# Attention, routing scores and experts in one block of engine programs, and the experts' parts added ahead of the shared part in 20 tiles

## What is computed

```python
x = layernorm(x + attention(x))              # 16 heads of 32, softmax over 1024 keys
scores = x @ gate_w.T                        # 8 experts
ew, ei = top_k(scores, 2); ew = softmax(ew)
routed = sum over the 2 chosen experts of ew * (silu(x @ w_gate.T) * (x @ w_up.T)) @ w_down.T
shared = (silu(x @ sh_gate.T) * (x @ sh_up.T)) @ sh_down.T
x = layernorm(x + routed + sigmoid(x @ se_gate_w.T) * shared)
```

## Time and profile before

| | us |
|---|---|
| median of 3 runs (2097.38 to 2098.63) | 2098.14 |
| the profiled execution | 2099.2 |
| its span, first to last instruction | 2097.5 |
| PE busy | 2018.8 (96%) |
| DVE busy | 1278.3 (61%) |
| ACT busy | 880.3 (42%) |
| POOL busy | 868.1 (41%) |
| granted TensorE clock, mean share of full | 0.988 |

### The profile page before, as it was taken

How to read it: one execution, slowest core, us unless ns; L and a number is a source line. 1 busy time by engine, 2 the same in 40 slices (tenths; PEclk the granted TensorE clock), 3 DMA queues, 4 the chain that set the end, 5 groups by cost and what they waited for, 6 DMA issues and landing times. The chain is left out here.

```text
span 2097.5 us, 30323 instructions
## 1 busy us (share of the span) xinstructions
PE 2018.8 (96%) x9764; PEld 1226.9 (58%) x9765; DVE 1278.3 (61%) x2281; ACT 880.3 (42%) x1563; POOL 868.1 (41%) x831
## 2 busy tenths in 40 slices
PE   7999999999999999999999986899999999999997
PEld 5655556655556655556655435588544444447886
DVE  5777775777776677775677855574222222225875
ACT  2266664466664466663466672321111111112332
POOL 3255654556654556653554555200111111114651
PEclk9999999999999999999999998999999999999999
DMA  7322434331434231335131305642222222225752
GB/s 231 71 53 55 100 78 107 115 69 42 101 76 131 92 76 47 97 67 163 60 77 33 91 12 201 221 186 66 90 90 88 86 87 89 90 80 166 229 175 74
DMA packets 95923, 213.00 MB, mean 102 GB/s; under 512 B 24305, under 2 KB 24817, under 8 KB 92593
## 3 DMA queue, kind: packets, MB, share of 16 engines
q1 hardware_dynamic: 84992, 175.96, 28.3%
q0 software_dynamic: 10800, 35.40, 6.2%
HBM read 118.51 MB, written 41.93 MB: 76 GB/s over the span
## 5 line engine op out<-in xcount | busy, mean ns | idle before, releaser
L947 DVE TENSOR_REDUCE max_half<-ps_side 128x1 f32<-128x512 f32 x1024 | 658.2, 682 | 204.6 <-PE ps_side L666 201.4
L666 PE MATMUL ps_side<-kq_stack 96*128 96x512 f32 x1024 | 409.4, 404 | 4.9 <-DVE max_half L947 2.4
L688 PE MATMUL ps_s<-kq_stack 97*128 97x512 f32 x937 | 393.0, 420 | 8.0 <-ACT probs_first L843 5.1
L688 PEld LDWEIGHTS ps_s<-kq_stack 97*128 97x128 f32 x937 | 177.8, 190 | 165.0 <-issue 85.5
L1636 PE MATMUL ps_gu<-gu_sb,xT_e 128*128 x568 | 257.7, 596 | 0.5 <-issue 0.3
L1534 POOL DMA_INDIRECT x_g<-x,who_all x71 | 67.3, 948 | 454.7 <-PE ps_t L1626 358.4
L843 ACT ACTIVATE probs_first<-ps_s 128x512 f32<-128x512 f32 x326 | 187.6, 600 | 106.0 <-PE ps_s L688 90.5
L666 PEld LDWEIGHTS ps_side<-kq_stack 96*128 96x128 f32 x1024 | 195.2, 191 | 57.8 <-DVE max_half L947 26.5
L843 ACT ACTIVATE probs_mid<-ps_s 128x512 f32<-128x512 f32 x308 | 177.5, 599 | 112.0 <-PE ps_s L688 97.4
L590 POOL TENSOR_TENSOR acc<-probs_first,probs_mid 128x512 f32<-128x512 f32 x129 | 163.8, 1297 | 133.2 <-ACT probs_mid L843 133.2
L843 ACT ACTIVATE probs_last<-ps_s 128x512 f32<-128x512 f32 x303 | 175.5, 599 | 97.2 <-PE ps_s L688 81.0
(11 more groups left out here) (237 smaller groups left out, 3312.0 us busy)
## 6 DMA issues: line engine op xcount, KB each, us to landing
kq_stack<-kq SPq DMA_DIRECT2D x192, 256.0 KB, 5.1
y_slots<-y_t SPq DMA_DIRECT2D x71, 256.0 KB, 2.3
x_r<-x SPq DMA_DIRECT2D x32, 256.0 KB, 3.7
x_t<-x SPq DMA_DIRECT2D x32, 256.0 KB, 2.9
gu_sb<-wgu SPq DMA_DIRECT2D x8, 1024.0 KB, 16.1
out<-gu_sb SPq DMA_DIRECT2D x32, 256.0 KB, 2.7
res<-inv_rows SPq DMA_DIRECT2D x124, 64.0 KB, 2.0
stage<-wkqT SPq DMA_DIRECT2D x28, 256.0 KB, 3.0
```

What stands on the lines that cost most here:

```text
L666: nc.tensor.matmul(bank, q_stack[par][0:3 * HD, h, t * P:(t + 1) * P], k_stack[par][0:3 * HD, h, half * HALF:(half + 1) * HALF], start=Tru ...
L688: nc.tensor.matmul(out, k_stack[par][0:3 * HD + 1, h, kt * P:(kt + 1) * P], q_stack[par][0:3 * HD + 1, h, half * HALF:(half + 1) * HALF], ...
L947: nc.vector.reduce_max(max_half[:, u // 2, u % 2:u % 2 + 1], bank, AX.X).then_inc(side_free, 1)
```

## The change

All of attention, scores and experts is put into one block: one program per engine, with no barrier between stages, and one identity matrix. What was in the block of the scores and now has to share memory with the attention became a class `Router`. Its buffers lie where those of `feed_forward` lie later.

Work that moves into the attention's last group and tail: POOL clears `rw_raw`; SP loads the kept projection weights (now into `kq_stack0`, at the start of group 3 in place of the end of group 1), `rw` and tiles 0 to 3 of x2; in the tail PE turns tiles 0 to 7, ACT and DVE split them, SP loads tiles 4 to 11 and the three shared weights. SP's orders in the last group and the tail:

```diff
+            def load_last(b):
+                sp.wait_ge(scores_ready, b * HEADS_B + (G - 1) * STEPS * HG)
+                sp.sem_inc(passed, 1)
+                for i, part in enumerate(wo_last):
+                    sp.dma_start(part.bitcast(F32), wo_kept[i]).then_inc(wo_in, 16)
+                sp.wait_ge(router.rw_zero, 1)
+                sp.dma_start(router.rw_raw[:, :, 0:E + 1], router.rw).then_inc(router.rw_in, 16)
+                for t in range(4):
+                    sp.wait_ge(x2_out[t], 16 * 2)
+                    load_r(t)
             def body(b, m, g, last):
+                if last and g == G - 1:
+                    load_last(b)
...
-                if last and g == 1:
-                    sp.wait_ge(proj_ready, PROJ * B * G)
-                    sp.sem_inc(passed_sp, 1)
-                    for i, part in enumerate((x_hi, x_lo)):
-                        sp.dma_start(part[:, :, 0:D].bitcast(F32), wo_kept[i]).then_inc(wo_in, 16)
...
+                sp.wait_ge(scores_ready, B * HEADS_B)
+                sp.sem_inc(passed, 1)
+                load_shared(0)
+                for t in range(3):
                     store(b, t)
+                for t in range(4, 8):
+                    sp.wait_ge(router.t_ready, t - 3)
+                    load_r(t)
+                    if t < 7:
+                        store(b, t - 1)
+                for t in range(8, 12):
+                    sp.wait_ge(router.t_ready, t - 3)
+                    load_r(t)
+                for t in range(6, KT):
+                    store(b, t)
+                for k in range(1, 3):
+                    load_shared(k)
+                for t in range(12, TT):
+                    if t >= (B - 1) * KT:
+                        sp.wait_ge(x2_out[t % KT], 16 * (B + 1))
+                    sp.wait_ge(router.t_ready, t - 3)
+                    load_r(t)
```

PE, ACT and DVE in the tail of the last batch, and the scores' groups, which no longer turn tiles 0 to 7:

```diff
             for t in range(KT):
                 o_tile(b * TAIL + KT + t, b, t, tail_bank(t),
-                       [x_hi[:, g, 0:D] for g in range(G)], [x_lo[:, g, 0:D] for g in range(G)])
+                       [wo_last[0][:, g, :] for g in range(G)], [wo_last[1][:, g, :] for g in range(G)])
...
+                if 3 <= t < KT - 1:
+                    router.turn(pe, 0, t - 3)
+            for s in range(4):
+                router.turn(pe, 1, s)
+            pe.wait_ge(tail_free, B * TAIL)
...
             for t in range(KT):
                 norm(B - 1, t)
+                if 1 <= t < 5:
+                    router.high(act, 0, 0, t - 1)
+                if t >= 5:
+                    for s in ((0, 1), (2, 3), ())[t - 5]:
+                        router.high(act, 1, 1, s)
...
+                if 3 <= t < KT - 1:
+                    router.low(dve, 0, 0, t - 3)
+            for s in range(4):
+                router.low(dve, 1, 1, s)
...
             def group(q, g, first, last):
+                if not first and not last:
+                    for s in range(4):
+                        r.turn(pe, q + 1, s)
```

In the experts' block SP loads its first four tiles while the scores still run, and the experts' weights (12 MB) when the last tile is turned; `up(0)` and `down(0)` wait for the split shared weights:

```diff
             for t in range(4):
+                sp.wait_ge(router.t_ready, TT - 3 + t)
                 load_tile(t)
+            sp.wait_ge(router.st_split, 3 * C)
+            sp.sem_inc(passed, 1)
...
+                if t == 0:
+                    pe.wait_ge(router.st_split, 2 * C)
```

In the last 20 tiles DVE adds both experts' rows to x first (`begin_combine`), in the step before the shared part is there, and then adds the shared part (`finish_combine`) straight from PSUM; `finish` and its buffer fall away for these tiles:

```diff
+            def begin_combine(t):
+                dve.wait_ge(x_in[t % 4], 16 * (t // 4 + 1))
+                add_experts(t, x_t[:, t % 4, :]).then_inc(begun, 1)
+
+            def finish_combine(t):
+                q = COMBINE_AT[t]
+                s = q % 4
+                dve.wait_ge(d_ready, t + 1)
+                dve.wait_ge(begun, t - COVER + 1)
+                nc.vector.scalar_tensor_tensor(out=res[:, s, :], in0=ps_d[:, t % 2, :], scalar=sgate_all[:, t:t + 1],
+                                               in1=res[:, s, :], op0=ALU.mult, op1=ALU.add).then_inc(added, 1)
+                statistics(q)
...
                 if i:
-                    finish(t - 1)
+                    finish_combine(t - 1)
                 h_low(t)
-                for what in COMBINE_STEPS[i]:
-                    combine(*what)
-            finish(TT - 1)
-            for what in COMBINE_STEPS[TT - COVER]:
-                combine(*what)
+                if i < COVER:
+                    combine_stored(i)
+                begin_combine(t)
+            finish_combine(TT - 1)
```

More of the change, by code:

```diff
@@ new lines, in __init__, with turn @@
+        self.x_in = [sem(f"xr_in{i}") for i in range(4)]
+        self.t_ready, self.t_hi, self.t_lo = sem("r_t_ready"), sem("r_t_hi"), sem("r_t_lo")
+        self.sc_ready, self.sc_taken = sem("sc_ready"), sem("sc_taken")
+        self.back_ready, self.sc_done = sem("back_ready"), sem("sc_done")
+        self.th_done, self.gate_done = sem("th_done"), sem("gate_done")
+    def turn(self, pe, q, s):
+        t = 4 * q + s
+        pe.wait_ge(self.x_in[s], 16 * (q + 1))
+        if not static(q, 1):
+            pe.wait_ge(self.t_hi, t - 3)
+            pe.wait_ge(self.t_lo, t - 3)
+        for c in range(C):
+            done = self.nc.tensor.transpose(self.ps_t[:, s, c * P:(c + 1) * P], self.x_t[:, s, c * P:(c + 1) * P],
+                                            self.ident[:])
+        done.then_inc(self.t_ready, 1)
@@ L1169, in _ @@
         def _(pe):
-            def turn(q, s):
-                t = 4 * q + s
-                pe.wait_ge(x_in[s], 16 * (q + 1))
-                if not static(q, 1):
-                    pe.wait_ge(t_hi, t - 3)
-                    pe.wait_ge(t_lo, t - 3)
-                for c in range(C):
-                    done = nc.tensor.transpose(ps_t[:, s, c * P:(c + 1) * P], x_t[:, s, c * P:(c + 1) * P], ident[:])
-                done.then_inc(t_ready, 1)
             def score(q, g):
@@ L1203, in group @@
             def group(q, g, first, last):
+                if not first and not last:
+                    for s in range(4):
+                        r.turn(pe, q + 1, s)
                 if first:
-                    for s in range(4):
-                        turn(q, s)
-                if not last:
-                    for s in range(4):
-                        turn(q + 1, s)
-                if first:
-                    pe.wait_ge(rw_split, 1)
+                    pe.wait_ge(r.rw_split, 1)
                 score(q, g)
@@ L1265, in group @@
             def group(q, g, first, last):
-                if first:
-                    low(q, g)
-                if not last:
-                    low(q + 1, 1 - g)
+                if not first and not last:
+                    for s in range(4):
+                        r.low(dve, q + 1, 1 - g, s)
                 take(q, g)
```

414 lines of the change are left out of this document (208 added, 206 removed).

## The result

The changed kernel takes **2083.38 us** (median of 5, 2078.27 to 2088.77) against 2098.63 in the same session: ratio 0.993, 95% interval 0.9907 to 0.9952, so 15.3 us faster where I had forecast 19.7. The median lies 0.4 us above the top of my range. The single times spread over 10.5 us, where the kernel before had spread over 2.4 (in the three later sessions it spread over 10.3, 8.8 and 5.6 itself). In microseconds the two intervals are 10.1 to 19.5 and 14.5 to 21.4 faster: my 19.7 lies just outside the first and inside the second, so the times alone can't tell which step of the forecast was off. The traces have to.

The account below looks back on a forecast made before the run. PE was taken to bound the kernel, with time to win only where it stands or runs at its lower clock. Gains of 14.1 + 4.3 + 0.5 + 0.8 = 19.7 off 2098.1 gave 2078.4 us, range 2073 to 2083.

Parts of the forecast that it names:

- D: Last 20 tiles, additions in a new order: shorter end, `h_low` of the last tile later; gain 0.8 us, bounds 0 and 1.6.
- What bounds the kernel: Whole kernel: PE is busy nearly throughout, so time comes off only where it stands still or runs at its lower clock.
- A: Tail of the attention to the third scoring group's end: eight tiles turned early; gain 14.1 us, bounds 11 and 19.
- B: End of the scores to up(0): tile already loaded, PE turns it at once; gain 4.3 us, bounds 1.7 and 4.3.
- C: Clock of up(0): it has just fallen when up(0) starts; gain 0.5 us, bounds 0 and 2.5.
- clock holds at up(0): At up(0): the clock does not fall, 2 us more gain, 2076.4 us; chance 0.24.
- slower rival: Last 20 tiles: stores landing at 8 us make `begin_combine`'s wait eat 25 us, 2103.5 us; chance 0.03.
- the longer wait: Tail of the attention: tile 12's load takes the full 10.1 us, gain there 11, 2081.5 us; chance 0.14.

Follow-up runs that it names:

- shift_pe: Changed kernel with 20 idle waits on PE alone ahead of the experts' loop; 2081.2 us, run once.
- late_turns: Changed kernel with turns, copies and subtractions of tiles 0 to 3 moved behind the attention's last projection, loads still early; 2084.12 us, ratio 0.9938.
- shift_act: Changed kernel with 20 idle waits on ACT alone ahead of the experts' loop; 2079.34 us, run once.
- combine_only: Kernel before the change with only the new order of the additions in the last 20 tiles; 2098.19 us, ratio 0.9995.

## Why the prediction was off, step by step

Two steps failed: part D, which left out what the longer wait does to the clock, and the experts' loop, which the sum put at nothing without a reason.

**What bounds the kernel** was read rightly: the gain lies where PE stood, and there it was found.

**A and B** together were put at 14.1 + 4.3 = 18.4. The profiled execution has 18.06, the eight traces with this tail 15.2 to 18.4, mean 17.3. The way there: the last norm ended at 1287.2 and not 1289.6, since ACT's waits for POOL ahead of the norms, 1.2 to 1.9 us each before the change, absorbed its extra copies; tile 7 was turned at 1285.2 and not 1287.7. The wait for tile 12 then was 4.19 us and not 3.0. I had the load on PE 8.8 us after the first of the two 1 MB issues, 1.2 us less than the 10.1 of before. It came 10.2 us after it (1287.60 to 1297.85), so that saving did not show in this trace, and it ate half of what came earlier ahead of it. The clock fell behind the wait, as the row had it. In this trace the turns start at 1297.85 (forecast 1298.9), and the third group's last product ends at about 1304.2 (1305.8); but 2.2 us of PE's lead were there before the tail, so A itself is near 13.5. B is right: from the last turned scores to up(0) 2.05 us, 2.0 forecast.

**C** was put at 0.5 with 2.5 as its bound, and both cases come, in one kernel: 0.85 in eight of twelve traces, 2.45 in four. "Has just fallen" costs less than I took from the one row. The rival "clock holds at up(0)" was real but moves the time by 1.6 us, not 2.

**D is the first step that failed.** I gave +0.8, bounds 0 and 1.6. I had the 1.6 us of the shorter end and the 0.8 us by which `h_low` comes later, and counted the latter as delay alone. But it lengthens PE's wait from 1.46 to 2.25 us, and behind that the clock falls, in seven of the nine traces with this order: another 1.6 us (1.2 in shift_pe, where it rose sooner), so -0.72. In late_turns and shift_act the clock held, and there D is +0.86 and +0.85, my figure. In part A I had priced a wait with the clock behind it; here I did not.

**The loop is the second: the sum left it at nothing.** The experts' loop, not named in it, lost 1.8 to 2.3 us in every joined program whose DVE code was not moved, 2.07 in the first: outside my sum, and larger than the D error of 1.5. The wait for stores in `begin_combine`, my slower rival, never showed: PE's time in the steps from the third to the last but one is that of before within 0.03 us. (That rival's time should read 2078.4 + 25 = 2103.4.)

**The account.** Against one execution: 18.06 + 2.45 - 2.07 - 0.72 for the change, +2.85 for what that execution of the kernel before had by itself, -1.47 in the second of the last 20 steps, of which it is open whether the change or that execution has it, and -0.65 in the attention, makes 18.4. Over the eight traces with this tail the change alone is about 17.3 (A, B) + 1.45 (C, mean) - 2.1 (loop) - 0.7 (D) = 16.0, between the 15.3 and 16.5 of the two sessions; were the second step's mean loss of 1.1 the change's own, it would be 14.9. Against my 19.7 that is: A and B -1.1, C +0.9, loop -2.1, D -1.5. The kernel before is no fixed mark either: combine_only, with its old tail, is 1.84 behind in A and B. My range took its slow end from A alone (the longer wait, 2081.5, and 1.5 of uncertainty), at 2083.0. The loop lay outside it, and D's loss outside D's bounds. That the first median missed the range by only 0.4 us is chance: executions differ by more.

**The spread** of 10 us: the mean granted clock of the five first runs falls from 0.995 (2078.27) to 0.991 (2087.9 and 2088.77). Time at the 1.2 GHz level is 2 (1 - clock) of the span, half of it lost; so 0.004 more of it is up to 8.3 us of the 10.5, an estimate (the clock is rounded to 0.001, which is 2 us, and time at the lower level in which PE stands costs nothing). Which places fall in the slowest executions is not known, as they have no profile. Those seen falling in some traces and holding in others are around 1015, at tile 16, at up(0) and in the last tile.

## What to carry to other kernels

When an edit makes TensorE's wait longer by under a microsecond near a place where the clock may fall, price the clock too: here 0.8 us of statistics in front of one subtraction cost 2.4. A transfer that ended a wait before will take back part of what is won ahead of it, so look what stands in front of it on the queue. Before a sum is made from one profiled execution, mark the stalls that a second one might not have, and after a change that moves all the code compare the loops it "does not touch" instruction by instruction.

## What had not been expected of the hardware

- The clock does not fall alike in equal situations. After the same 2.25 us wait before the last products it fell in seven traces and held in two; at up(0), after the same 1.46 us wait and the short transposes before it, it fell in eight and held in four. At 1240 it fell behind a wait of 3.0 us and held behind one of 2.7.
- DVE's first work after the loop's jump back was 0.12 us later in the joined program, 0.36 at the first jump, and 20 idle waits ahead of the loop took that away: 2.1 us over 16 jumps, within 0.3 us in every trace. That it is the place of the code is inferred from these waits.
- ACT's `act_g` in the second of the last 20 steps starts 2.0 to 3.6 us after PE has gone on to the next transposes in 13 of 14 traces, and 0.2 us in the one of the kernel before, with or without a fetch of instructions nearby. PE loses 0.6 to 2.9 us there. The cause is open.
